# One core, conditioned FFN: first x turned on TensorE, loads reordered, small weights in long rows

## What is computed

```python
q_emb = relu(q @ W3 + b3)                              # cond 64x256 -> 64x512
v = (n * x + sum_over_tokens(x)) * q_emb[:, None, :]   # n = 64
y = relu(v @ W2 + b2)
base   = y @ W_base + b_base
shared = (y @ A_s) @ B_s                               # rank 16
gates  = softmax(y @ W_router + b_router)              # 6 experts, the top 2 kept
routed = sum_e gate_e * (y @ A_r[e]) @ B_r[e]          # rank 16 each
out = x + base + shared + routed
```

## Time and profile before

| | us |
|---|---|
| device time, median of 3 runs | 247.85 |
| lowest and highest run | 246.45, 248.17 |
| the profiled execution: device time | 246.59 |
| the profiled execution: span on the core | 244.9 |
| PE busy in it | 235.0 (96%) |
| DVE busy in it | 177.4 (72%) |
| ACT, POOL busy in it | 102.1, 55.7 |

### The profile page before, as it was taken

One profiled execution on the slowest core, in us unless ns is written; L12 is line 12 of the kernel. 1 busy time (PEld: TensorE's weight loads), 2 busy tenths in 40 slices (PEclk: granted clock), 3 DMA queues, 4 the chain that ended last, 5 costly groups with the idle time before them and its releaser, 6 DMA issues.

```text
span 244.9 us, 3159 instructions
## 1 busy us (share of the span) xinstructions
PE 235.0 (96%) x1007; PEld 189.4 (77%) x1007; DVE 177.4 (72%) x324; ACT 102.1 (42%) x206; POOL 55.7 (23%) x58
## 2 busy tenths in 40 slices
PE   7699599999999999999999999999999999999994
PEld 2577378888887878888888888888888888888883
DVE  0697898869988996679766995679756995351344
ACT  2247557234434445245533455145433455134330
POOL 5078971202312041012302121012202121000000
PEclk9769979999999999999999999999999999999999
DMA  7989990818016368019610567018000530013004
GB/s 151 299 198 208 270 249 1 170 69 280 0 58 116 146 200 171 0 43 299 143 33 0 183 197 137 0 43 300 0 0 0 192 150 0 0 53 120 3 0 173
DMA packets 32219, 28.49 MB, mean 116 GB/s; under 512 B 6173, under 2 KB 22621, under 8 KB 32206
## 3 DMA queue, kind: packets, MB, share of 16 engines
q1 hardware_dynamic: 32050, 28.33, 42.9%
q10 hardware_dynamic: 156, 0.00, 0.0%
HBM read 19.94 MB, written 8.39 MB: 116 GB/s over the span
## 4 chain that ended last, share of the span: by engine, by line
PE 69%; DVE 16%; SPq 6%; DMA 4%; issue 2%; POOL 1%; ACT 1%; POOLq 0%; DVEq 0%
PE m_ps L661 61%; PE hT L661 7%; DMA x_quart<-in_x_dram 4%; DVE xT L424 4%; DVE out_nat L548 3%; DVE x_sum L438 3%; SPq L217 2%; DVE vsum L429 2%; DVE y_lo L452 2%; SPq L205 1%; POOL x_full L284 1%; DVE x_lo L446 1%; SPq L211 1%; PE hT L748 1%; ACT x_hi L321 1%
## 5 line engine op out<-in xcount | busy, mean ns | idle before, releaser
L284 POOL TENSOR_TENSOR x_full<-x_sum,qT 128x512 f32<-128x512 f32 x31 | 37.9, 1222 | 138.5 <-DVE x_sum L438 138.5
L661 PE MATMUL m_ps<-Wb_lo,y_hi 128*128 128x512 f32 x128 | 50.1, 391 | 0.0
L661 PE MATMUL m_ps<-Wb_hi,y_lo 128*128 128x512 f32 x128 | 50.1, 391 | 0.0
L661 PE MATMUL m_ps<-Wb_hi,y_hi 128*128 128x512 f32 x128 | 50.0, 391 | 0.0
L661 PE MATMUL m_ps<-x_hi,W_hi 128*128 128x512 f32 x112 | 43.8, 391 | 0.2 <-DVE x_lo L446 0.2
L661 PE MATMUL m_ps<-x_lo,W_hi 128*128 128x512 f32 x112 | 43.6, 389 | 0.0
L661 PE MATMUL m_ps<-x_hi,W_lo 128*128 128x512 f32 x112 | 43.6, 389 | 0.0
L329 ACT ACTIVATE y_full<-m_ps,b_sb 128x512 f32<-128x512 f32 x32 | 22.0, 688 | 49.3 <-PE m_ps L661 46.4
L424 DVE STREAM_TRANSPOSE xT<-x_quart 128x512 f32<-128x512 f32 x32 | 34.8, 1088 | 7.6 <-DMA x_quart<-in_x_dram 7.6
L452 DVE TENSOR_TENSOR y_lo<-y_full,y_hi 128x512 fp32r<-128x512 f32 x32 | 25.0, 780 | 12.5 <-ACT y_hi L331 12.5
L446 DVE TENSOR_TENSOR x_lo<-x_full,x_hi 128x512 fp32r<-128x512 f32 x32 | 22.9, 719 | 10.9 <-ACT x_hi L321 10.9
(11 more groups left out here) (82 smaller groups left out, 263.7 us busy)
## 6 DMA issues: line engine op xcount, KB each, us to landing
x_quart<-in_x_dram SPq DMA_DIRECT2D x32, 256.0 KB, 4.8
x_nat<-in_x_dram SPq DMA_DIRECT2D x8, 1024.0 KB, 6.0
out_dram<-out_nat SPq DMA_DIRECT2D x32, 256.0 KB, 2.1
W_f<-in_L_cond_W_dram SPq DMA_DIRECT2D x4, 256.0 KB, 6.3
Wb_f<-in_L_ffn_W_base_dram SPq DMA_DIRECT2D x1, 1024.0 KB, 7.0
W_sb<-in_L_cond_W_dram SPq DMA_DIRECT2D x1, 512.0 KB, 6.0
Wd_f<-in_L_ffn_A_r_dram SPq DMA_DIRECT2D x4, 48.0 KB, 3.1
Wu_f<-in_L_ffn_B_r_dram SPq DMA_DIRECT2D x1, 192.0 KB
```

The source lines that it names most:

```text
L284: nc.gpsimd.tensor_tensor(per_batch(x1_full[:, c, :]), per_batch(x1_sum[:, c, :]), qT[:, c, bass.ds(BG * g, BG)].unsqueeze(2).to_broadcast ...
L661: mm = nc.tensor.matmul(psum, lhsT, rhs, start=start and i == 0, stop=stop and i == len(terms) - 1)
```

## The change

- SP loads `x_nat` of group 0 first, tile by tile (four DMAs, rows of 2 KB), then W3, W2, the small weights, Wb, b2 and group 1's quarters. Group 0 has no quarters. cond goes on ACT's queue. Group 2's quarters and group 1's `x_nat` wait for nothing.
- PE turns group 0's x: 16 transposes of 128 x 128 into four PSUM banks `head_ps`, with idle matmuls between token tiles.
- DVE sums, adds and scales group 0's x in PSUM (`sum_head`, `scale_head`; the add writes PSUM in place), and scales all four chunks itself; before, POOL scaled three of them.
- The features of y are numbered 4p+k (partition p, chunk k): Wb, b2, router, A_s and A_r load in rows four times as long, into raw tiles `Ar_f`, `As_f`, `Wr_f` that are split by three instructions each. The columns of W2 are put in that order when it is split (`by_tile`).
- `m1_first`: chunks 0 and 1 by chunk as before; chunks 2 and 3 tile pair by tile pair. The last q product (c = 3) comes after chunk 0.
- Two of four Wb remainders move from POOL to DVE, behind group 0's x_lo and ahead of group 1's turn.
- 7, 1, 1, 1 and 5 idle matmuls in place of 12, 6 and 3.

```diff
-    WARM_LOAD, WARM_COPY, WARM_SPLIT = 12, 6, 3
+    WARM_LOAD, WARM_TILE, WARM_W3 = 7, 1, 5
...
-        q_ps = [hT, m2_ps[0], m2_ps[1], m2_ps[3]]
+        q_ps = m1_ps[:KC - 1] + [m2_ps[0]]
+        head_ps = [m2_ps[0], m2_ps[1], m2_ps[3], hT]
...
+        def by_tile(ap):
+            return ap.rearrange("p (j m) -> p m j", m=KC)
+        def in_tiles(ap):
+            return ap.rearrange("p (m j) -> p m j", m=KC)
+        def Wd_parts(wide):
+            return (wide[:, :, RO:P].rearrange("p k (e r) -> p k e r", r=R), wide[:, :, SH:SH + R], wide[:, :, 0:E])
+        Wd_raw = (Ar_f[:, :, :, :].rearrange("p e k r -> p k e r"), As_f[:, :, :], Wr_f[:, :, :])
...
@@ SP @@
-            load_quarters(0, 0)
-            sp.dma_start(cond_sb[:, :], cond).then_inc(cond_loaded, 16)
+            for t in range(TT):
+                sp.dma_start(x_nat[0][:, t, :], x_groups[0][:, t, :]).then_inc(head_loaded[t], 16)
             sp.dma_start(W3_sb[:, :, :], W3.rearrange("(k p) d -> p k d", p=P)).then_inc(W3_loaded, 16)
             for c in range(KC):
                 sp.dma_start(W2_f[:, c, :], W2.rearrange("(p c) n -> p c n", c=KC)[:, c, :]).then_inc(W2_loaded[c], 16)
-            sp.dma_start(b2_sb[:, :], b2.rearrange("(k p) -> p k", p=P), allow_slow_non_contiguous=True).then_inc(b2_loaded, 16)
-            sp.wait_ge(zeroed, 4)
-            sp.dma_start(Wd_f[:, :, 0:E], W_router.rearrange("(k p) e -> p k e", p=P)).then_inc(Wd_loaded, 16)
-            sp.dma_start(Wd_f[:, :, SH:SH + R], A_s.rearrange("(k p) r -> p k r", p=P)).then_inc(Wd_loaded, 16)
-            for k in range(KC):
-                sp.dma_start(Wd_f[:, k, RO:P].rearrange("p (e r) -> p e r", r=R),
-                             A_r[:, k * P:(k + 1) * P, :].rearrange("e p r -> p e r")).then_inc(Wd_loaded, 16)
-            sp.dma_start(Wb_f[:, :, :], W_base.rearrange("(k p) d -> p k d", p=P)).then_inc(Wb_loaded, 16)
+            sp.dma_start(Ar_f[:, :, :, :], A_r.rearrange("e (p k) r -> p e k r", k=KC)).then_inc(Wd_loaded, 16)
+            sp.dma_start(As_f[:, :, :], A_s.rearrange("(p k) r -> p k r", k=KC)).then_inc(Wd_loaded, 16)
+            sp.dma_start(Wr_f[:, :, :], W_router.rearrange("(p k) e -> p k e", k=KC)).then_inc(Wd_loaded, 16)
+            sp.dma_start(Wb_f[:, :, :], W_base.rearrange("(p k) d -> p k d", k=KC)).then_inc(Wb_loaded, 16)
+            sp.dma_start(b2_sb[:, :], b2.rearrange("(p m) -> p m", m=KC)).then_inc(b2_loaded, 16)
             load_quarters(1, 1)
+            sp.wait_ge(zeroed, 3)
...
-            sp.dma_start(x_nat[0][:, :, :], x_groups[0]).then_inc(x_loaded[0], 16)
...
@@ SP, step @@
-                    sp.wait_ge(xT_ready, KC * g + KC)
+                    if not first:
+                        sp.wait_ge(xT_ready, turned(g, KC - 1))
...
@@ POOL @@
-            for c in range(KC):
-                if c:
-                    pool.wait_ge(qT_ready, c + 1)
-                    scale(0, c)
-                W_rest(W2_lo[:, c, :], W2_f[:, c, :], W2_hi[:, c, :], c + 1, W2_lo_ready)
-            W_rest(Wd_lo[:, :, :], Wd_f[:, :, :], Wd_hi[:, :, :], KC + 1, Wd_lo_ready)
-            for k in range(KC):
-                W_rest(Wb_lo[:, k, :], Wb_f[:, k, :], Wb_hi[:, k, :], KC + 2 + k, Wb_lo_ready)
+            for c in range(KC):
+                pool.wait_ge(W2_hi_ready, c + 1)
+                W_rest(in_tiles(W2_lo[:, c, :]), by_tile(W2_f[:, c, :]), in_tiles(W2_hi[:, c, :]), W2_lo_ready)
+            for n, (lo, raw, hi) in enumerate(zip(Wd_parts(Wd_lo), Wd_raw, Wd_parts(Wd_hi))):
+                pool.wait_ge(Wd_hi_ready, n + 1)
+                W_rest(lo, raw, hi, Wd_lo_ready)
+            for k in range(KC // 2):
+                pool.wait_ge(Wb_hi_ready, k + 1)
+                W_rest(Wb_lo[:, k, :], Wb_f[:, k, :], Wb_hi[:, k, :], Wb_lo_ready)
...
@@ ACT @@
+            act.dma_start(cond_sb[:, :], cond).then_inc(cond_loaded, 16)
...
+            q_relu(0)
+            W2_split(0)
+            q_relu(1)
+            x1_split(0, 0, 0)
+            q_relu(2)
+            W2_split(1)
+            x1_split(0, 0, 1)
+            W2_split(2)
+            W2_split(3)
+            x1_split(0, 0, 2)
+            q_relu(3)
+            act.wait_ge(Wd_loaded, 16 * 3)
+            for hi, raw in zip(Wd_parts(Wd_hi), Wd_raw):
+                nc.scalar.activation(hi, raw, ACT.Copy).then_inc(Wd_hi_ready, 1)
+            x1_split(0, 0, 3)
             act.wait_ge(Wb_loaded, 16)
             for k in range(KC):
-                if k == KC // 2:
-                    x1_split(0, 0, KC - 1)
...
@@ DVE @@
+            def sum_head(c):
+                dve.wait_ge(head_turned, c + 1)
+                nc.vector.tensor_reduce(vsum_head[:, c, :], per_batch(head_ps[c][:, :]), AX.X,
+                                        ALU.add).then_inc(vsum_head_ready, 1)
+                dve.wait_ge(vsum_head_ready, c + 1)
+                nc.vector.scalar_tensor_tensor(
+                    out=per_batch(head_ps[c][:, :]), in0=per_batch(head_ps[c][:, :]), scalar=float(N),
+                    in1=vsum_head[:, c, :].unsqueeze(2).to_broadcast([P, BG, N]),
+                    op0=ALU.mult, op1=ALU.add).then_inc(x1_sum_ready, 1)
+            def scale_head(c):
+                dve.wait_ge(qT_ready, c + 1)
+                dve.wait_ge(x1_sum_ready, c + 1)
+                nc.vector.tensor_tensor(per_batch(x1_full[:, c, :]), per_batch(head_ps[c][:, :]),
+                                        qT[:, c, 0:BG].unsqueeze(2).to_broadcast([P, BG, N]),
+                                        ALU.mult).then_inc(x1_full_ready, 1)
+            sum_head(0)
+            sum_head(1)
+            scale_head(0)
+            scale_head(1)
             x1_rest(0, 0, 0)
+            sum_head(2)
+            scale_head(2)
+            x1_rest(0, 0, 1)
+            sum_head(3)
+            scale_head(3)
+            x1_rest(0, 0, 2)
+            x1_rest(0, 0, 3)
+            for k in range(KC // 2, KC):
+                dve.wait_ge(Wb_hi_ready, k + 1)
+                nc.vector.tensor_tensor(Wb_lo[:, k, :], Wb_f[:, k, :], Wb_hi[:, k, :].bitcast(F32),
+                                        ALU.subtract).then_inc(Wb_lo_back_ready, 1)
...
@@ PE @@
-            keep_warm(WARM_COPY)
+            for t in range(TT):
+                pe.wait_ge(head_loaded[t], 16)
+                for c in range(KC):
+                    turn = nc.tensor.transpose(head_ps[c][:, t * P:(t + 1) * P],
+                                               x_nat[0][:, t, :].rearrange("p (f c) -> p c f", c=KC)[:, c], ident[:, :])
+                    if t == TT - 1:
+                        turn.then_inc(head_turned, 1)
+                keep_warm(WARM_TILE if t < TT - 1 else WARM_W3)
...
@@ PE, m1_first @@
-                for k in range(KC - 1):
+                for k in range(KC // 2):
...
+                    if k == 0:
+                        pe.wait_ge(x1_full_ready, 1)
+                        q(KC - 1)
+                for tiles in ((0, 1), (2, 3)):
+                    for k in range(KC // 2, KC):
+                        pe.wait_ge(x1_hi_ready, k + 1)
+                        pe.wait_ge(W2_lo_ready, k + 1)
+                        for m in tiles:
+                            chunk(m, k, W2_hi, x1_hi)
+                            chunk(m, k, W2_lo, x1_hi)
+                            pe.wait_ge(x1_lo_ready, k + 1)
+                            last = chunk(m, k, W2_hi, x1_lo)
```

More of the change, by code:

```diff
@@ L280, in scale @@
                 pool.wait_ge(x1_sum_ready, n + 1)
-                if not (isinstance(g, int) and g == 0):
-                    pool.wait_ge(x1_lo_ready, n + 1 - KC)
+                pool.wait_ge(x1_lo_ready, n + 1 - KC)
                 nc.gpsimd.tensor_tensor(per_batch(x1_full[:, c, :]), per_batch(x1_sum[:, c, :]),
@@ L432, in add_sum @@
             def add_sum(g, c):
-                n = KC * g + c
-                dve.wait_ge(vsum_ready, n + 1)
-                if not (isinstance(g, int) and g == 0):
-                    dve.wait_ge(x1_full_ready, n + 1 - KC)
+                dve.wait_ge(vsum_ready, turned(g, c))
+                dve.wait_ge(x1_full_ready, KC * g + c + 1 - KC)
                 nc.vector.scalar_tensor_tensor(
@@ L676, in m1, with q @@
                 mm.then_inc(m1_done, 1)
+            def q(c):
+                for k in range(QC):
+                    mm = nc.tensor.matmul(q_ps[c][:, 0:B], W3_sb[:, k, :].rearrange("p (f c) -> p c f", c=KC)[:, c],
+                                          condT[:, k, :], start=(k == 0), stop=(k == QC - 1))
+                mm.then_inc(q_done, 1)
             def m1_first():
@@ L751, in _ @@
             pe.wait_ge(condT_copied, 1)
-            for c in range(KC):
-                for k in range(QC):
-                    mm = nc.tensor.matmul(q_ps[c][:, 0:B], W3_sb[:, k, :].rearrange("p (f c) -> p c f", c=KC)[:, c],
-                                          condT[:, k, :], start=(k == 0), stop=(k == QC - 1))
-                mm.then_inc(q_done, 1)
```

(3 more changed lines are left out.)

85 lines of the change are left out of this document (39 added, 46 removed).

## The result

The changed kernel took 248.2 us (median of 15 runs, 247.58 to 248.75), the kernel before, run beside it, 246.98 us (15 runs, 246.45 to 248.17). The ratio is 1.0043, with a 95% interval from 1.0028 to 1.0058: slower by 0.4%, by my bound no change that counts, and 6 us above the forecast of 242.1, outside its range. The profiled execution took 248.67 us for a span of 246.9 (before: 246.59 and 244.9).

A forecast was written before the change was run, and what follows sets the result against it. PE, busy 96% of the span, was taken as the bound, with only the head able to move: first y_lo done at 8.3 + 17.5 = 25.8 instead of 30.9 gains 5.1 us, from 247.2 to 242.1 us; range 239.3 to 245.2.

The follow-up runs named there:

- b_shift: The kernel before with one unused 32-byte tensor declared ahead of Wu_f; 251.41 us, ratio 1.0206 to the kernel before.
- b_m1only: The kernel before with 32 unused bytes ahead of W2_hi and 224 behind W2_lo; 248.6 us beside 247.84 before, one run each.
- b_w2only: The kernel before with a 32-byte pad ahead of W2_hi and another behind W2_lo; 250.77 us beside 246.82 before, one run each.

## What to carry to other kernels

Where PE is the bound, look up where the two operands of its products stand in SBUF: here distances of 32, 64, 96 and 128 bytes per partition (modulo 256) gave a mean pitch of 232.5 to 233.7 ns in place of 226.7, some 3%, and a pad of 32 bytes was enough (b_shift). Compare the start-to-start time of the same products before and after each change, since neither the granted clock nor the busy share showed it (1.00, and 27.00 of 27.00 us, from 92 to 119 us of both kernels). And when work is made strided to save a transfer, ask which engine's queue stands behind the two that pay for the stride.

## What the hardware showed that I had not expected

Distances of 32, 96 and 128 bytes modulo 256 between the operands of a 128x128 by 128x512 float32r product gave a mean of 233.2, 233.7 and 232.5 ns from start to start, a distance of 0, 256 or both operands shifted alike 226.7 ns, at the same granted clock of 1.00; products of other pairs in the same kernel were untouched (b_m1only: m1 233.1, m2 226.7 ns). A distance of 64 is shown by m2 and h in b_w2only, 233.2 and 233.3 ns; the few products of `up`, at 64 as well, had 229.2. A split on ACT that reads every fourth of 128x512 elements took 1.12 us against 0.62, and POOL's subtraction 1.70 against 1.45 with the same neighbours. W3's products, 64 columns of plain float32, start 0.233 us apart at a granted clock of 0.50 (kernel before) and at 1.00 (changed kernel).
